# A cross-attention and mixture-of-experts kernel on one core: one-piece loads with a reordered start, and the first expert blocks inside the last steps over the tiles

## The reference

```python
q = layernorm(x) @ Wq.T + bq; k = ctx @ Wk.T + bk; v = ctx @ Wv.T + bv
s = where(mask == 0, -1e9, q.k / sqrt(16))               # per head, 77 keys
x1 = x + softmax(s) @ v @ Wo.T + bo
h = x1 + (layernorm(x1) * ln1_g + ln1_b) @ attn_w.T
t = layernorm(h) * ln2_g + ln2_b
top_vals, top_idx = top_k(t @ gate_w.T, 2); rw = softmax(top_vals)
for e in 0..7:
    oe = (silu(t @ gate_proj[e].T) * (t @ up_proj[e].T)) @ down_proj[e].T   # inner width 1024
    out += rw_of_e * oe                                  # 0 for tokens that did not choose e
result = h + out
```

## Time and profile before

| | us |
|---|---|
| median of 3 runs | 586.43 (585.51, 586.43, 589.74) |
| profiled execution, its own time | 586.9 |
| its span | 585.3 |
| PE busy in the span | 521.6 (89%) |
| DVE busy | 350.4 (60%) |
| POOL busy | 257.9 (44%) |

### The profile page before, as it was taken

The page is one execution under the profiler, slowest core; times in us unless marked ns, Lnnn a source line. Parts: engine busy times, 40 slices in busy tenths (PEclk is TensorE's granted clock), DMA queues, the critical chain, the costliest instruction groups (busy, mean ns, idle before and its releaser), DMA issues.

```text
span 585.3 us, 14031 instructions
## 1 busy us (share of the span) xinstructions
PE 521.6 (89%) x3389; PEld 448.9 (77%) x3390; DVE 350.4 (60%) x805; ACT 260.9 (45%) x523; POOL 257.9 (44%) x429
## 2 busy tenths in 40 slices
PE   2579999999998639999998999999999999999992
PEld 1367888888887428888887888887888888978882
DVE  2877889888786447543468456438433465385630
ACT  0445757675654223232375254336232363466420
POOL 5251445555455574564433525443543434432222
PEclk9858979999898658999999999999999999999997
DMA  7730010101010146621101455360162101530000
GB/s 219 205 141 2 18 37 20 36 20 36 18 36 20 37 153 132 227 81 45 46 27 36 150 190 201 101 202 27 44 212 77 45 27 45 169 112 29 20 17 27
DMA packets 25607, 48.10 MB, mean 82 GB/s; under 512 B 10560, under 2 KB 18652, under 8 KB 25440
## 3 DMA queue, kind: packets, MB, share of 16 engines
q1 hardware_dynamic: 15552, 33.55, 18.0%
q0 software_dynamic: 7360, 13.19, 7.4%
q10 hardware_dynamic: 2656, 0.91, 0.7%
HBM read 39.30 MB, written 9.39 MB: 83 GB/s over the span
## 4 chain that ended last, share of the span: by engine, by line
PE 73%; DVE 10%; issue 6%; POOL 3%; ACT 3%; DMA 2%; SPq 0%; POOLq 0%; DVEq 0%; ACTq 0%
PE psum L1305 18%; PE psum L1306 17%; PE psum L1307 17%; PE psum L1354 5%; PE psum L1202 4%; PE psum L1186 4%; DVE s_max L867 2%; PE psum L1225 2%; PE psum L1181 2%; DMA wk<-in_wkT 2%; DVE s_sb L873 1%; PE psum L1260 1%; PE psum L1324 1%; PE psum L1219 1%; ACT tT L768 1%
## 5 line engine op out<-in xcount | busy, mean ns | idle before, releaser
L1305 PE MATMUL psum<-split_w,tb_hi 128*128 x288 | 117.6, 408 | 6.6 <-issue 5.9
L1306 PE MATMUL psum<-split_w,tb_hi 128*128 x288 | 113.3, 393 | 0.0
L1307 PE MATMUL psum<-split_w,tb_lo 128*128 x288 | 113.2, 393 | 0.0
L1305 PE MATMUL psum<-split_w,aT_hi 128*128 x288 | 84.3, 293 | 3.2 <-DVE aT_lo L1129 3.1
L687 POOL DMA_INDIRECT out_x<-o_sb,add_at x36 | 36.4, 1012 | 110.8 <-DVE o_sb L1121 107.7
L1306 PE MATMUL psum<-split_w,aT_hi 128*128 x288 | 81.3, 282 | 0.0
L1307 PE MATMUL psum<-split_w,aT_lo 128*128 x288 | 81.2, 282 | 0.0
L1129 DVE TENSOR_TENSOR aT_lo<-psum,aT_hi 128x512 fp32r<-128x512 f32 x72 | 46.3, 684 | 55.9 <-ACT aT_hi L813 55.9
L843 DVE TENSOR_TENSOR split_w<-split_w (+1 forms) x48 | 56.1, 1218 | 31.8 <-ACT split_w L792 31.8
L1305 PEld LDWEIGHTS psum<-split_w,tb_hi 128*128 128x128 f32 x288 | 54.8, 190 | 18.2 <-issue 8.5
L1307 PEld LDWEIGHTS psum<-split_w,tb_lo 128*128 128x128 f32 x288 | 54.5, 189 | 11.5
(11 more groups left out here) (175 smaller groups left out, 957.9 us busy)
## 6 DMA issues: line engine op xcount, KB each, us to landing
split_w<-in_experts SPq DMA_DIRECT2D x28, 768.0 KB
split_w<-in_experts SPq DMA_DIRECT2D x1, 3072.0 KB
x_sb<-in_x SPq DMA_DIRECT2D x8, 256.0 KB, 5.5
...
blk<-lists POOLq DMA_DIRECT2D x36, 1.0 KB, 2.1
rows<-z_rows,gather_at POOLq DMA_INDIRECT x36, 3.1
```

What stands on the lines that cost most here:

```text
L1305: nc.tensor.matmul(dst, hi, w_hi, start=first, stop=False)
L1306: nc.tensor.matmul(dst, hi, w_lo, start=False, stop=False)
L1307: return nc.tensor.matmul(dst, lo, w_hi, start=False, stop=last)
```

## The change

It has two parts. **The start:** every load comes in one piece with longer rows (the inputs are laid out for that on the host), in another order, with a semaphore of its own each, so that PE waits for each weight where it uses it. The v product on PE moves behind the first scores (step 2), v_heads on DVE behind the softmax of tile 0. Of the moments of x, groups 1 and 2 move behind `chunk_values` (step 3), group 3 to step 4. The bias is added on DVE in place of POOL, once ahead of the steps and at steps 4, 5 and 6. Most splits of expert 0's weights move one step later. One small activation is run at the very start (L769 of the new kernel).

**The end of the tiles:** four early blocks in place of three, whose lists are read after tile 8 in place of tile 12 (SOON_TILES 9). SP loads the lists behind the store of tile 11; POOL waits for them at step 17, gathers the rows of blocks 0 and 1 there, the sums so far at step 18, the rows of block 2 at step 20 and of block 3 at step 21. PE transposes rows 0 and 1 at step 18, makes gate and up of block 0 at step 19, those of block 1 and the transposes of block 0's activations at step 20, the down product of block 0 and the transposes of block 2's rows at step 21. The expert pipeline then begins at its step 3. The router's weights of tiles 14 and 15 (an exponential on ACT, a reciprocal and a product on DVE) move to step 22. Fourteen fills with zeros of 128 KB are added on SP's queue, since blocks whose list is read early point at rows not yet written. `row_table`, `block_tables` and `due_tables` move to expert steps 3, 3 and 4.

```diff
-SOON, SOON_TILES = 3, 13
-BLOCKS = FULL_BLOCKS + EXPERTS - 1 + SOON
+SOON, SOON_TILES, FIRST_BLOCKS = 4, 9, 6
+BLOCKS = FULL_BLOCKS + EXPERTS - 1 + FIRST_BLOCKS
...
-FIRST_HIGH = {3: (0, 1), 4: (2,), 5: (3,), 6: (4,), 7: (5,)}
-FIRST_LOW = {4: (0, 1), 5: (2,), 6: (3,), 7: (4,), 8: (5,)}
+FIRST_HIGH = {4: (0, 1), 5: (2,), 6: (3, 4), 7: (5,)}
+FIRST_LOW = {5: (0, 1), 6: (2,), 7: (3, 4), 8: (5,)}
...
             def load_x(i):
-                for b in range(BATCH):
-                    sp.dma_start(x_sb_pairs[:, 2 * i:2 * i + 2, b, :], x_tiles[:, 2 * i:2 * i + 2, b, :]).then_inc(x_in[i], 16)
-
+                sp.dma_start(x_sb[:, GROUP * i:GROUP * (i + 1), :], x[:, GROUP * i:GROUP * (i + 1), :]).then_inc(x_in[i], 16)
+
+            sp.dma_start(wk_sb[:, :, :], wkT).then_inc(wk_in, 16)
             load_x(0)
-            for w, src, done in ((wv_sb, wvT, wkv_in), (wk_sb, wkT, wkv_in), (wq_sb, wqT, wqo_in)):
-                sp.dma_start(w[:, :, :], src.rearrange("(k p) n -> p k n", p=P)).then_inc(done, 16)
+            sp.dma_start(wq_sb[:, :, :], wqT).then_inc(wq_in, 16)
+            sp.dma_start(wv_sb[:, :, :], wvT).then_inc(wv_in, 16)
             load_x(1)
-            for w, src, done in ((wo_sb, woT, wqo_in), (aw_sb, awT, aw_in), (gw_sb, gwT, aw_in)):
-                sp.dma_start(w[:, :, :], src.rearrange("(k p) n -> p k n", p=P)).then_inc(done, 16)
-
-
+            sp.dma_start(wo_sb[:, :, :], woT).then_inc(wo_in, 16)
+            sp.dma_start(aw_sb[:, :, :], awT).then_inc(aw_in, 16)
+            sp.dma_start(gw_sb[:, :, :], gwT).then_inc(gw_in, 16)
+
+
+            load_x(2)
+            load_x(3)
             sp.wait_ge(v_done, BATCH)
...
-            load_x(2)
-            load_x(3)
...
+                if number_is(t, SOON_TILES + SCATTER - LN2 - 1):
+                    soon_lists()
+
+            def soon_lists():
+
+                for par in range(2):
+                    sp.wait_ge(listed[par], 16 * TOPK * ((SOON_TILES + 1 - par) // 2))
+                for n in range(SOON):
+                    sp.dma_start(blk[:, n], lists[n * P:(n + 1) * P, :]).then_inc(soon_in, 16)
+
+            for t in range(SOON_TILES, TILES):
+                sp.dma_start(z2_tiles[t // 2, t % 2], zeros[:, :]).then_inc(pad_out, 16)
+                sp.dma_start(out_tiles[t // 2, t % 2], zeros[:, :]).then_inc(blank_out, 16)
...
-                if isinstance(number(t0), int) and number(t0) < GROUPS:
-                    root_x(number(t0))
-                    add_bias(number(t0))
+                if number_is(t0, 0):
+                    root_x(0)
...
                 if number_is(t8, SOON_TILES):
-                    soon_rows()
+                    pool.wait_ge(soon_in, 16 * SOON)
...
+                if number_is(it, PV):
+                    root_x(1)
+                    root_x(2)
+                if number_is(it, PV + 1):
+                    root_x(3)
+                if number_is(t8, SOON_TILES):
+                    soon_rows()
+                if number_is(t8, SOON_TILES + 1):
+                    soon_sums()
+                if number_is(t5, LAST):
+                    pool.wait_ge(z2_out[0], 16 * TILES // 2)
+                    pool.wait_ge(tT_ps, TILES - 1)
+                    gather_rows(2, 2)
+                if number_is(t6, LAST):
+                    pool.wait_ge(z2_out[1], 16 * TILES // 2)
+                    pool.wait_ge(tT_ps, TILES)
+                    gather_rows(3, 3)
...
+            nc.scalar.activation(warm[:, 1:2], warm[:, 0:1], ACT.Identity)
...
+                if within(t7, TILES) and not in_drain(t7):
+                    second_weight(t7)
...
+                if number_is(t3, LAST):
+                    rows_T(early[0])
+                    rows_T(early[1])
+                if number_is(t4, LAST):
+                    second_weight(back(it, MIX))
+                    gated(0, early[0])
+                    gated(1, early[0])
+                if number_is(t5, LAST):
+                    gated(0, early[1])
+                    acts_T(early[0])
+                    gated(1, early[1])
+                if number_is(t6, LAST):
+                    rows_T(early[2])
+                if number_is(t7, LAST):
+                    second_weight(back(it, LIST + 1))
+                    second_weight(t7)
```

And on DVE (the constants and masks moved with the groups are left out) and PE:

```diff
-                if number_is(it, QK + 1) or number_is(it, PV + 1):
-                    shift_of(number(it) - 1)
...
+                if number_is(it, QK):
+                    values()
+                if number_is(it, PV + 1):
+                    shift_of(1)
+                    shift_of(2)
+                if number_is(it, PV + 2):
+                    shift_of(3)
...
+            def add_bias(i):
+
+                dve.wait_ge(x_in[i], 16)
+                dve.wait_ge(bo_in, 16)
+                nc.vector.tensor_tensor(x1_sb[:, GROUP * i:GROUP * (i + 1), :], x_sb[:, GROUP * i:GROUP * (i + 1), :],
+                                        bo_sb[:, :].unsqueeze(1).to_broadcast([P, GROUP, D]), ALU.add).then_inc(xb_done, 1)
...
-            moments_x(1)
-            shift_of(1)
...
+            shift_of(0)
+            dve.wait_ge(mask_in[0], 16)
+            nc.vector.tensor_scalar(masked[:, 0:GROUP, :], mask_i[:, 0:GROUP, :], 0.0, NEG, ALU.is_equal, ALU.mult).then_inc(mask_done, 1)
+            add_bias(0)
...
-                        pe.wait_ge(v_done, BATCH)
                         pe.wait_ge(mask_done, 1)
...
+                if number_is(it, QK):
+                    values()
...
+                if number_is(t3, LAST):
+                    rows_T(early[0])
+                    rows_T(early[1])
...
+                if number_is(t4, LAST):
+                    pe.wait_ge(s_done, 2 * TILES)
+                    pe.wait_ge(topi_done, DRAIN)
+                    pe.wait_ge(w_ready, PARTS)
+                    pe.wait_ge(tbl_done, 1)
+                    gate_up(0, early[0], first_weights())
+                    gate_up(1, early[0], first_weights())
+                if number_is(t5, LAST):
+                    pe.wait_ge(tbl_done, 2)
+                    gate_up(0, early[1], first_weights())
+                    pe.wait_ge(h_done, TILES)
+                    pe.wait_ge(place_done, DRAIN)
+                    acts_T(early[0])
+                    gate_up(1, early[1], first_weights())
+                if number_is(t6, LAST):
+                    pe.wait_ge(x1_done, TILES)
+                    pe.wait_ge(place_done, LAST)
+                    down(early[0], first_weights())
+                    pe.wait_ge(topi_done, TILES)
+                    rows_T(early[2])
...
+                if number_is(it, 3):
+                    pe.wait_ge(before_done, TILES)
+                    pe.wait_ge(y_done, 1)
+                    nc.tensor.matmul(small[1], ones[:, :], before[:, 0, :], start=True, stop=True).then_inc(cnt_ps, 1)
...
+                if number_is(it, 3):
+                    pe.wait_ge(tab, 1)
```

395 lines of the change are left out of this document (228 added, 167 removed).

## The result

The changed kernel is slower: 600.23 us (median of 4 runs, 597.68 to 604.78) against 587.16 for the kernel before, ratio 1.0241 [1.0187, 1.0294] (the bracket is a 95% interval). 582 was forecast, with 573 to 590 as the range. The profiled execution is the longest of the four (604.78, span 603.2), so its times are read here beside those of the two parts of the change, each run alone: "start alone" and "end alone" are the first two experiments.

| | before | after | start alone | end alone |
|---|---|---|---|---|
| o_rec of tile 0 | 43.65 | 35.55 | 35.04 | 43.55 |
| o_rec of tile 5 | 95.13 | 90.08 | 90.93 | 94.99 |
| choice of tile 15 | 212.73 | 223.60 | 208.53 | 223.54 |
| last scatter issued | 221.91 | 235.89 | 217.72 | 235.84 |
| list of block 4 (before and start alone: 3) issued | 231.09 | 243.39 | 227.64 | 242.83 |

A forecast was written before the change was run, and what follows sets the result against it. PE was taken to bound the kernel, with 73% of the chain of waits (DVE 10%). 586.9 - 6.2 (start) + 1.4 (end of the tiles) = 582.1, less 0.5 to the median: 581.6, rounded to 582 us; range 573 to 590.

The forecast's parts named there:

- behind it nothing changes: After the down product of block 3: the remaining expert work and program end were taken to add no time.
- The shift: DVE at the start: the 128x4 shift of 2.31 us, held by POOL's bias addition, falls to about 0.2 us.
- v as what ends last: Start: v's trip through memory sets o_rec of tile 0, with v back at 28.1 us, or 30.5 at worst.
- given back: Tiles from 43.65 to 95.13 us: DVE's added work takes back 3.2 us, between nothing and 5.8.
- The first softmax: DVE at the start: begins at 17.8 us in place of 24.57, with PE's scores taken as ready.
- The wait for the early lists: POOL, last tiles: waits for lists loaded behind the store of tile 11, taken as 1.7 us.
- 24 products stand on PE ahead of the rank of tile 13: PE, last tiles: early products take 5.4 us, 1.0 of it beside waits, so 4.4 us of delay.
- the wait of PE for the down product of block 3: PE, early blocks: it comes early to this product and waits some 8 us, because later blocks need the list.
- The low clock behind that wait: PE, down product of block 3: at most ten products at the lower clock, 2 us, half counted, 1.0.
- the slower rival: Early blocks on PE run at the lower clock: 9.5 us more for two gate-ups, 591 us in all; chance 0.10.
- the lists did not come in time: Judges the rival with block 4's list loaded at 232.6 and block 3's down product 5.4 earlier: 575 us; chance 0.25.
- the 1.4 to 2.5 of the second: Rival on the start: its gain is mostly swallowed, 1.4 to 2.5 us stay, 586 us in all; chance 0.20.

The follow-up runs named there:

- down late, tables early: Changed kernel with block 0's down product and block 2's rows behind the tiles, count, row and block tables at step 22, both early gate-ups kept: 598.58 us.

## Why the prediction was wrong

Two steps failed at the end of the tiles, side by side: the row table was taken as ready, and the chain to the last scatter was sized at half of what it became. A third, "behind it nothing changes", failed by itself. The start was right in most of its steps and too large.

**The start: right in most steps, too large in its sum.** The shift, the bias (1.22 for an estimated 1.2) and v as what ends last came as said, and 3.1 us were given back by tile 5, for 3.2; that DVE's added work took them was not tried. The first softmax came at 18.94, near the forecast 17.8, but by luck: that time was the length of DVE's list, and DVE was through with it at 13.7 and waited 5.25 us for PE's scores, which the prediction took as ready. o_rec of tile 0 came at 35.55 in place of 34.2: v_heads ended at 22.77 for a forecast 21.6, and v's trip from there to v_chunks took 7.3 us, between the 6.5 taken and the 8.85 kept as the bad end. The trace of the start alone shows 4.2 left of the forecast 6.2 at block 3, the medians 2.6 (584.09 against 586.65).

**The tiles' end: one gate-up was counted where more stand in the way.** The forecast, in the times of before, had the choice of tile 15 7.4 us later and the last scatter 7.5; in "end alone", which has none of the start's gain, they come 10.8 and 13.9 later (223.54, 235.84). The wait for the early lists was sized well, 1.7 us for a measured 1.4. The step "24 products stand on PE ahead of the rank of tile 13", 4.4 us, was not: block 1's 24 products stand ahead of the rank of tile 14 too, and block 0's down product ahead of that of tile 15. In "end alone" the choices of tiles 13, 14 and 15 come 3.8, 7.1 and 10.8 later than before. The weight of tile 15 was put 5.2 us behind its choice and comes 7.3 behind it (230.91 and 223.60 in the changed kernel), since its exponential on ACT stands behind the rows of block 2 and these on PE behind the down product; in "down late, tables early", where rows and down product have moved, it comes 1.0 behind the choice, and the last scatter is issued at 226.57. The price of the two gate-ups with the tables early is 6.3 us, partly by the low clock, which the slower rival had as its mechanism. By its own sign it did not hold: the granted clock was 0.76 from block 0's first product to its last (199.46 to 206.67 us) and 0.68 in block 1's stretch (211.16 to 220.45), not near 0.5; its price for both blocks was 9.5.

**The list of block 4: the step that failed beside it.** The prediction let the list hang on the landing of the last scatters alone and took the row table as ready. The diff shows that `row_table` and `block_tables` go to expert step 3; that move was costed at nothing without a look at what then stands ahead of the count on PE. The list came at 242.83 in "end alone" for a forecast of 237, where the landed scatters alone would have let it go at about 240.7 (238.9 and the 1.8 that it follows the later of the two), and with the scatters out of the way it still came at 243.14. Once the first table was back, the second held the third list in the same way. What comes behind the list was right: 23.7 us from it to the weighting of block 2 were forecast, 23.4 were measured in "end alone", and the wait of PE for the down product of block 3 was 6.15 for some 8. The low clock behind that wait was sized at ten products and 1.0 us; in the changed kernel all 24 products of that down product are 0.21 apart or more, in place of 0.12, some 2 us.

**"Behind it nothing changes": the third step that failed.** The change's own constant adds three bodies under conditions to the programs of four engines. That they run for no token was taken as no cost; they cost 6.1 us. Of the two places that the prediction named for a hidden cost, the stage behind block 3 has the 2 us of above, and the fills show nothing beyond that.

**The sum.** The end part was forecast at +1.4 and is +15.4 alone: 6.1 for the skipped bodies, some 8 for the tables and the early products together (600.23 to 592.30), and the rest, 1.4, is near the 2 us behind block 3. The first two were measured with the start in place, so that the sum is an estimate. Of the rivals none was it: the lists did not come in time; the slower one had a mechanism that is seen for a part of the products; and the start's gain by the medians, 2.6, is close to the 1.4 to 2.5 of the second, though its sign, a stretch from o_rec of tile 0 to tile 5 that grows by more than 6 us, did not show (3.1).
